# Attention and quantised feed-forward block on one core: another order of the shared work, and another split of the PSUM banks

## What is computed

```python
xn = layernorm(x)
Q, K, V = xn @ W_q.T, xn @ W_k.T, xn @ W_v.T      # 16 heads of 16
scores = rope(Q) @ rope(K).T * DH ** -0.5          # causal
heads = softmax(scores) @ V
attn = heads @ W_o.T
xq, wq = fake_quant_fp8(xn), fake_quant_fp8(weight)   # one scale per tensor
out = x + attn + (xq @ wq.T + bias)
```

## The kernel before

| slot | items | slot | items |
|---|---|---|---|
| 0, 2 | v0; v1 | 11 | fin0 |
| 1, 7 | mt1; mt2 | 12 | at2, mt3 |
| 3 to 6 | o0; o1; o2; o3 | 13 | qk2 |
| 8 | at0, qk0 | 14 | fin1, at3 |
| 9 | at1 | 15, 16 | qk3; fin2, mt0 |
| 10 | qk1 | 17, 18, 19 | none; fin3; none |

## Time and profile before

### The profile page before, as it was taken

The page is one execution under the profiler, slowest core; times in us unless marked ns, Lnnn a source line. Parts: engine busy times, 40 slices in busy tenths (PEclk is TensorE's granted clock), DMA queues, the critical chain, the costliest instruction groups (busy, mean ns, idle before and its releaser), DMA issues.

```text
span 438.0 us, 9484 instructions
## 1 busy us (share of the span) xinstructions
PE 384.9 (88%) x2990; PEld 205.9 (47%) x2990; DVE 355.3 (81%) x1380; ACT 290.6 (66%) x487; POOL 245.4 (56%) x266
## 2 busy tenths in 40 slices
PE   7998987878879988998899898989899998898886
PEld 7685543333434544454445444545445433353335
DVE  3899679999888988898888979887989797879104
ACT  3529538567765777587866776676677677669751
POOL 5444263365559548556666666676666565245750
PEclk9996979999989999999999999999999999999999
DMA  8944032302503143302630262018031613020111
GB/s 280 307 146 71 1 94 79 73 2 97 123 0 75 52 157 62 75 27 94 148 75 1 98 171 61 15 52 216 15 62 49 183 38 74 2 99 4 49 49 49
DMA packets 27810, 36.40 MB, mean 83 GB/s; under 512 B 3984, under 2 KB 25872, under 8 KB 26320
## 3 DMA queue, kind: packets, MB, share of 16 engines
q1 hardware_dynamic: 27760, 35.79, 30.2%
HBM read 22.94 MB, written 12.58 MB: 81 GB/s over the span
## 4 chain that ended last, share of the span: by engine, by line
PE 63%; ACT 16%; DVE 10%; issue 7%; POOL 2%; DMA 1%; ACTq 0%; POOLq 0%; SPq 0%; DVEq 0%
PE o_ps L1047 15%; ACT prob L803 12%; PE st_ps L943 9%; PE m_ps L927 9%; PE m_ps L1005 7%; PE m_ps L982 7%; PE s_ps L962 5%; DVE scratch L657 4%; PE m_ps L989 2%; PE s_ps L899 2%; DVE prod L605 2%; DMA q_st<-shift 1%; PE m_ps L1013 1%; DVE prod L604 1%; DVE amax L593 1%
## 5 line engine op out<-in xcount | busy, mean ns | idle before, releaser
L803 ACT ACTIVATE prob<-st_ps,exp_scale 128x512 f32<-128x512 f32 x320 | 202.9, 689 | 98.9 <-PE st_ps L943 98.2
L657 DVE CUSTOM_DVE_ANT_0 scratch<-s_ps,causal 128x512 bf16<-128x512 f32 (+3 forms) x512 | 221.3, 484 | 35.8 <-PE s_ps L962 33.8
L510 POOL TENSOR_SCALAR_AFFINE_SELECT prob<-prob 128x512 f32<-128x512 f32 (+1 forms) x160 | 90.1, 565 | 147.4 <-ACT prob L803 147.3
L943 PE MATMUL st_ps<-q_st,k_st 50*128 50x128 f16 (+3 forms) x512 | 108.9, 303 | 35.4 <-ACT prob L803 26.9
L962 PE MATMUL s_ps<-k_st,q_st 48*128 48x512 f16 (+3 forms) x512 | 109.7, 306 | 4.7 <-DVE rowmax L657 4.4
L943 PEld LDWEIGHTS st_ps<-q_st,k_st 50*128 50x128 f16 x512 | 35.2, 94 | 121.1 <-ACT prob L803 74.6
L1047 PE MATMUL o_ps<-prob,v_sb 128*17 128x512 f32 (+3 forms) x1024 | 82.8, 441 | 1.7 <-POOL prob L510 0.9
L962 PEld LDWEIGHTS s_ps<-k_st,q_st 48*128 48x128 f16 x512 | 34.5, 95 | 15.9 <-DVE rowmax L657 9.0
L657 DVE DVE_READ_ACCUMULATOR2_ANT rowmax<- 128x1 f32 x512 | 41.1, 80 | 0.0
L1047 PEld LDWEIGHTS o_ps<-prob,v_sb 128*17 128x17 f32 x1024 | 23.2, 97 | 30.0 <-issue 23.0
L982 PE MATMUL m_ps<-wv_sb,xnT 128*128 128x256 f32 x128 | 33.7, 408 | 1.5 <-ACT v_sb L810 1.3
(11 more groups left out here) (130 smaller groups left out, 493.5 us busy)
## 6 DMA issues: line engine op xcount, KB each, us to landing
qk_parts<-parts SPq DMA_DIRECT2D x14, 512.0 KB, 3.6
xnT<-x_dram SPq DMA_DIRECT2D x8, 512.0 KB, 8.5
q_st<-qk_parts SPq DMA_DIRECT2D x15, 256.0 KB, 4.2
k_st<-qk_parts SPq DMA_DIRECT2D x15, 256.0 KB, 4.6
x_res<-x_dram SPq DMA_DIRECT2D x7, 512.0 KB, 3.4
out_dram<-x_res SPq DMA_DIRECT2D x7, 512.0 KB, 3.0
q_st<-qk_parts SPq DMA_DIRECT2D x17, 128.0 KB, 3.2
k_st<-qk_parts SPq DMA_DIRECT2D x17, 128.0 KB, 4.9
```

The costliest lines, as they stand in the source:

```text
L510: eng.affine_select(out=ap, in_=ap, compare_op=ALU.is_ge, fill=0.0, base=0, pattern=pat, channel_multiplier=-1).then_inc(masked, 1)
L657: eng.tensor_tensor_reduce(scratch[:, at % 3, col:col + w], s_ps[at % 3][:, col:col + w], causal[:, T - w:T], 1.0, NEG, ALU.add, ALU.max, ...
L803: eng.activation(prob[u][:, half * T:(half + 1) * T], st_ps[ST_BANK[2 * s + half]][:, :], ACT.Exp, scale=exp_scale[:, 0:1]).then_inc(exp_d ...
L943: mm = eng.matmul(st_ps[ST_BANK[i]][:, col:col + T - kb * P], k_rows(n, h, ROWS + SHIFT, slice(kb * P, (kb + 1) * P)), q_rows(n, h, ROWS + ...
```

## The change

Shared items get new slots, the attention transposes go two to a bank (`at` 0 and 1), `fin` 2 and 3 of a batch move to slots 2 and 5 of the batch after next (for batch 6, LAST_FINS keeps all four in batch 7), and v 0 of a batch moves into the last slot of the batch before. In slots 0 to 19 taken modulo 20 the items now stand like this:

| slot | items | slot | items |
|---|---|---|---|
| 0 | v1 | 10 | qk0 |
| 1 | mt1 | 11 | mt3 |
| 2 | fin2 | 12 | qk1 |
| 3 | o0 | 13 | at1 (row blocks 2, 3) |
| 4 | o1 | 14 | fin1 |
| 5 | fin3 | 15 | qk2 |
| 6 | mt2 | 16 | mt0 |
| 7 | o2, at0 (row blocks 0, 1) | 17 | qk3 |
| 8 | o3 | 18 | none |
| 9 | fin0 | 19 | v0 |

st_ps gets 3 banks and s_ps 2, so an attend waits for the exponential three banks back and a compare for the maxima two banks back. v_sb, x_res and xq are doubled and attnT holds all four row blocks. The steps of CHAIN, of the quantisation, of the residual and of SyncE's stores move with the items.

```diff
-OFFSETS = {("v", 0): 0, ("mt", 1): 1, ("v", 1): 2, ("o", 0): 23, ("o", 1): 24, ("o", 2): 25, ("o", 3): 26, ("mt", 2): 7,
-           ("at", 0): 28, ("qk", 0): -32, ("at", 1): 29, ("qk", 1): -30, ("fin", 0): 31, ("at", 2): 32, ("mt", 3): 12,
-           ("qk", 2): -27, ("fin", 1): 34, ("at", 3): 34, ("qk", 3): -25, ("fin", 2): 36, ("mt", 0): -4, ("fin", 3): 38}
+OFFSETS = {("v", 0): -1, ("v", 1): 0, ("mt", 0): -4, ("mt", 1): 1, ("mt", 2): 6, ("mt", 3): 11,
+           ("o", 0): 23, ("o", 1): 24, ("o", 2): 27, ("at", 0): 27, ("o", 3): 28, ("at", 1): 33,
+           ("fin", 0): 29, ("fin", 1): 34, ("fin", 2): 42, ("fin", 3): 45,
+           ("qk", 0): -30, ("qk", 1): -28, ("qk", 2): -25, ("qk", 3): -23}
+LAST_FINS = {("fin", 0): 29, ("fin", 1): 30, ("fin", 2): 34, ("fin", 3): 35}
-CHAIN = {("rotate", 0): -29, ("high", 0): -28, ("low", 0): -26, ("write", 0): -25, ("rotate", 1): -24, ("high", 1): -23,
-         ("low", 1): -21, ("write", 1): -20, ("read", 0, 0): -19, ("read", 0, 1): -16, ("read", 1, 0): -12,
-         ("read", 1, 1): -11}
+CHAIN = {("rotate", 0): -27, ("high", 0): -26, ("low", 0): -24, ("write", 0): -22, ("rotate", 1): -22, ("high", 1): -21,
+         ("low", 1): -19, ("write", 1): -17, ("read", 0, 0): -16, ("read", 0, 1): -14, ("read", 1, 0): -8,
+         ("read", 1, 1): -6}
...
-ST_BANK = [i % 2 for i in range(HALVES)]
-ST_BEFORE = [i - 2 for i in range(HALVES)]
+ST_BANKS, S_BANKS = 3, 2
...
-    first, last, loop = (24, 25, 26, 27, 28), (6, 7, 11, 12, 14), (16, 17, 21, 22, 24)
+    first, last, loop = (24, 25, 26, 27, 28), (6, 7, 11, 12, 14), (16, 18, 20, 23, 25)
...
-        v_sb = sb("v_sb", [P, NQ, H, VW])
+        v_sb = sb("v_sb", [P, 2, NQ, H, VW])
-        scratch = sb("scratch", [P, 3, T], BF16)
+        scratch = sb("scratch", [P, S_BANKS, T], BF16)
-        attnT = sb("attnT", [P, 2, NC, P])
-        x_res = sb("x_res", [P, NQ, D])
-        xq = sb("xq", [P, NC, T], BF16)
+        attnT = sb("attnT", [P, NQ, NC, P])
+        x_res = sb("x_res", [P, 2, NQ, D])
+        xq = sb("xq", [P, 2, NC, T], BF16)
...
-                for g, off in enumerate((-3, 2, 8, 13)):
+                for g, off in enumerate((-3, 2, 7, 12)):
...
-                n = batch_at(slot, 39)
-                if n is not None and n < NB - 1:
-                    store(n)
+                for n in range(NB - 1):
+                    if slot == SLOTS * n + (47 if n < NB - 2 else 37):
+                        store(n)
...
-                n = batch_at(slot, -34, 2)
+                n = batch_at(slot, -32, 2)
                 if n is not None:
                     split_x(n)
...
-                n = residual_at(slot, 29, 17)
+                n = residual_at(slot, 27, 17)
...
-                    wait_past(eng, exp_done, HALVES * n + ST_BEFORE[i] + 1)
+                    wait_past(eng, exp_done, HALVES * n + i - ST_BANKS + 1)
...
-                    wait_past(eng, max_done, ITEMS * n + (ITEMS_UP_TO[f - 3] if f >= 3 else ITEMS_UP_TO[f - 3] - ITEMS))
+                    wait_past(eng, max_done, ITEMS * n + (ITEMS_UP_TO[f - S_BANKS] if f >= S_BANKS else ITEMS_UP_TO[f - S_BANKS] - ITEMS))
...
+            def turn_two(n, i, bank):
+                turn_attn(n, 2 * i, bank, 0)
+                return turn_attn(n, 2 * i + 1, bank, D)
```

More of the change, by code:

```diff
@@ L68, in schedule @@
     order = {key: i for i, key in enumerate(OFFSETS)}
-    items = [(EARLY[kind, k] if (kind, n) == ("qk", 1) else SLOTS * n + off, order[kind, k], kind, n, k)
+    items = [(EARLY[kind, k] if (kind, n) == ("qk", 1) else
+              SLOTS * n + (LAST_FINS[kind, k] if (kind, n) == ("fin", NB - 2) else off), order[kind, k], kind, n, k)
              for (kind, k), off in OFFSETS.items() for n in range(NB) if (kind, n) != ("qk", 0)]
@@ L218, in xq_of, with residual_of @@
         def xq_of(n):
-            return xq if n < NB - 1 else parts[:, 0, 0].bitcast(BF16)
+            return xq[:, n % 2]
+        def residual_of(n):
+            return x_res[:, n % 2]
         def q_rows(n, h, rows, cols):
@@ L244, in attention_ffn_block @@
                         for i in range(2)]
-        wf_sb = xq[:, :, :].rearrange("p c t -> p (c t)").bitcast(F32).rearrange("p (c n) -> p c n", c=NC)
-        st_ps = [pb(f"st_ps{i}", [P, T]) for i in range(2)]
-        s_ps = [pb(f"s_ps{i}", [P, T]) for i in range(3)]
+        wf_sb = xq[:, 0].rearrange("p c t -> p (c t)").bitcast(F32).rearrange("p (c n) -> p c n", c=NC)
+        st_ps = [pb(f"st_ps{i}", [P, T]) for i in range(ST_BANKS)]
+        s_ps = [pb(f"s_ps{i}", [P, T]) for i in range(S_BANKS)]
         o_ps = pb("o_ps", [P, T])
@@ L253, in attention_ffn_block @@
         first_ps = m_ps + s_ps[0:2]
-        tail_o, tail_at = s_ps + m_ps[0:1], m_ps[1:2] + st_ps + [o_ps]
+        tail_o, tail_at = s_ps + m_ps, st_ps + [o_ps]
         turn_ps = (st_ps[0], o_ps)
@@ L808, in copy_v @@
                 if i == 0:
-                    wait_past(eng, pv_done, 8 * n)
-                eng.copy(v_sb[:, 2 * i:2 * i + 2, :, 0:DH],
+                    wait_past(eng, pv_done, 8 * (n - 1))
+                eng.copy(v_sb[:, n % 2, 2 * i:2 * i + 2, :, 0:DH],
                          bank[:, :].rearrange("p (k h w) -> p k h w", k=2, h=H)).then_inc(v_copied, 1)
@@ L817, in copy_heads, with copy_at, copy_last_at @@
                 eng.copy(heads[:, g, :], o_ps[:, :]).then_inc(heads_copied, 1)
[L819 to L828 removed]
+            def copy_at(n, i, bank):
+                eng.wait_ge(full["at"], 2 * n + i + 1)
+                wait_past(eng, full["fin"], 4 * (n - 1) + 2 * i + 2)
+                eng.copy(attnT[:, 2 * i:2 * i + 2], bank[:, :].rearrange("p (q c n) -> p q c n", q=2, c=NC))\
+                   .then_inc(at_copied, 1)
+            def copy_last_at(qb, bank):
+                n = NB - 1
+                eng.wait_ge(full["at"], 2 * n + qb + 1)
+                eng.wait_ge(full["fin"], 4 * n)
+                eng.copy(attnT[:, qb], bank[:, 0:D].rearrange("p (c n) -> p c n", c=NC)).then_inc(at_copied, 1)
             nw = NC * D
@@ L848, in _ @@
                     eng.wait_ge(w_max_done, 8)
-                n = batch_at(slot, -35, 2)
+                n = batch_at(slot, -34, 2)
                 if n is not None:
@@ L877, in _ @@
                     copy_v(n, i, shared["v", n, i])
-                for n, qb in [(n, qb) for _, n, qb in shared_at(slot, "at")]:
-                    copy_at(n, qb, shared["at", n, qb])
+                for n, i in [(n, i) for _, n, i in shared_at(slot, "at")]:
+                    copy_at(n, i, shared["at", n, i])
                 for g in range(NG - 1):
@@ L898, in keep_busy @@
                 for _ in range(count):
-                    eng.matmul(s_ps[2][:, 0:P], ident[:, :], ident[:, :], start=True, stop=True)
+                    eng.matmul(st_ps[2][:, 0:P], ident[:, :], ident[:, :], start=True, stop=True)
             def turn_rows(n):
@@ L1004, in output_of_attn @@
                 for c in range(NC):
-                    mm = eng.matmul(bank[:, 0:D], attnT_of(n, qb)[:, c, :], wo_sb[:, c, :],
+                    mm = eng.matmul(bank[:, 0:D], attnT[:, qb, c, :], wo_sb[:, c, :],
                                     start=(first and c == 0), stop=(not first and c == NC - 1))
```

64 lines of the change are left out of this document (22 added, 42 removed).

## The result

The change makes the kernel **slower**: 455.58 us median of four runs (453.69 to 457.13) against 440.38 for the kernel before, run beside it on the same chip (439.63 to 443.50). The ratio is 1.033, with a 95% interval of 1.026 to 1.040. The forecast was 424, its range 412 to 437; the time lies on the other side of no change, next to the 454 of the fourth rival, but mostly not by that rival's mechanism.

A forecast was written before the change was run, and what follows sets the result against it. TensorE was taken to bound the kernel, standing still 5.75 us of each 46.15 us batch. Start +2.5, batch 1 -3.0, batches 2 to 5 -8.8, batch 6 -2.9, batch 7 -3.4 sum to -15.6 from 439.77: 424 us, range 412 to 437.

The forecast's parts named there:

- fourth rival: Every slot: two s_ps banks couple VectorE and TensorE, a batch takes 48.6 us, in all 454 us; chance 0.12.
- I take +2.5, bounds +1 and +5: Start and batch 0: back-to-back v items and two s_ps banks leave VectorE idle, slot 19 ends 2.4 us later.
- It gains 2.2 too: Batch 1: the steady batch's 2.2 us gain plus 0.8 for fin 2 and 3 leaving it, 3.0 in all.
- only remove waits: Whole kernel: doubling xq, x_res and v_sb was costed at nothing, as it could only take waits away.
- 43.95 us a batch: Batches 2 to 5: 40.4 us of TensorE work plus 3.55 of new stops; 2.2 less each, 8.8 for four.
- so ScalarE's hold on TensorE goes: Steady batches: a third st_ps bank and even items remove all of the 5.75 us standstill except the listed new stops.
- Together 2.55: Steady batch: compares wait for VectorE's maxima, 1.1 us after slots 10, 12, 15, 1.0 in slot 19, 0.45 after slot 4.
- The wait in slot 8: Slot 8: first_block waits for o_ps behind ScalarE's heads copy, itself held until o 3; 0.7 us of standstill.
- The collision: Slot 18: VectorE's exponent step qe meets GpSimd's rotation; 0.3 us a batch, bounds 0 and 1.
- second rival: Slot 18 of six batches: the port lock decides, 1.2 us in place of 0.3, in all 429 us; chance 0.10.
- -2.9 and -3.4: Batch 6 forecast at 38.7 us, 2.9 less; batch 7 at 37.1, 3.4 less, with the tail from 424.4 us unchanged.
- The marks I had set: Confirming: st_ps hold under 2 us, slot 20 2 to 3 later. Refuting: batches above 45.5, s_ps waits above 5, qk0 waiting.

The follow-up runs named there:

- e3: Changed kernel with ScalarE's copy of v in slot 20 moved ahead of its four weight scalings: 451.48 us, 1.020 of the kernel before.
- e7: Changed kernel on the old banks (two st_ps, three s_ps), with slot 20's v copy first and batch 0's quantisation early: 435.85 us, 0.988 of the kernel before.
- e9: e7 with batch 0's residual loaded in slot 4 and biased in slot 13, before the exponents: 435.25 us, 0.987 of the kernel before.
- e11: e7 with the attends from slot 150 on cycling over all five score banks: median 439.24 us over ten runs, 0.983 of the kernel before.
- e12: e7 with the edits of e9, e10 and e11 together: 432.79 us, 0.985 of the kernel before.
- e10: e7 with o 2 and o 3 one slot earlier and at 0 one later: 438.24 us, 0.994 of the kernel before.
- e13: e7 with the edits of e9 and e11, without that of e10: 432.02 us, 0.977 of the kernel before.
- e6: e5 on the old banks, two st_ps and three s_ps: 437.09 us, 0.990 of the kernel before.
- e2: Changed kernel on the old banks (two st_ps, three s_ps), so the new order alone: 445.54 us, 1.009 of the kernel before.
- e8: Changed kernel with the first matmul of each attend of batch 0 issued twice: 454.69 us, 1.031 of the kernel before.
- e4: Changed kernel with batch 0's last two quantisation steps moved to slot 26, ahead of the residual's addition and split_x: 449.73 us, 1.017 of the kernel before.
- e5: Changed kernel with the edits of e3 and e4 and batch 0's v items in slots 0 and 2: 447.16 us, 1.015 of the kernel before.
- two-by-two: Old and new order, each on old and new banks; steady batch 46.2 (both old), 47.5 (e1), 44.2 (e2), 45.4 us (both new).
- e14: Changed kernel with VectorE's exponent step qe moved from slot 18 back to slot 17: 460.71 us, 1.044 of the kernel before.
- e1: Kernel before with only the banks moved (three st_ps, two s_ps), old order kept: 453.69 us, 1.026 of the kernel before.

## Why the prediction was wrong, point by point

1. **The start and batch 0: the step that failed most by size.** I wrote "I take +2.5, bounds +1 and +5". Slot 20 is reached at 122.26 in place of 108.36, 13.9 later. Three things are in it. ScalarE's copy behind the scalings is 3.7 (e3 reaches slot 20 at 118.56). The banks are 2.9 to 3.9 (e3 against the 114.7 to 115.7 of e7, e9, e11 and e12, which also have the copy first and a slow first v). The other 6.3 to 7.3 is the new order in an execution with a slow first v; in e10 and e13, where that product was fast, slot 20 is reached at 111.3, only 3.0 later than before. So 3.3 to 4.4 of it can come and go with the execution, which I had not priced. The kernel before had a slow first v (3.78), and I counted with that figure, so like against like the order costs 6.3 to 7.3; that my +2.5 is near the 3.0 of the fast kind is luck. Which waits make up the 6.3 to 7.3 no run splits. Of the cause I looked at the wrong half: the v items back to back, which e6 against e7 shows to be worth nothing on the old banks. I had two s_ps banks leave VectorE dry twice (0.35 and 1.25) and put no stop of TensorE behind VectorE in batch 0, where VectorE is the fuller engine: matmuls for s_ps wait 9.3 us there, in 20 places, weight loads 15.0, against 1.7 and 2.8 before, and the run of value products at 80.73 takes 2.76 us where the four steady ones take 1.49. My roll by slots priced every later item at the higher level. The grant of 0.83 isn't the banks' alone: on the old banks batch 0 had 0.86 in e2 and e7 and 0.82 in e9, with 49.4 us. How much of the loss is waiting and how much is clock stays open (e8).

2. **Batch 1: "It gains 2.2 too", 3.0 in all, was +6.4, and the stop of 3.64 in front of it +3.6.** I moved `fin` 0 of batch 0 five slots forward, as the list has it, and didn't follow xq back through GpSimd's queue; nor did I look at what stands ahead of copy_v in slot 20 on ScalarE. Both stops were readable from the diff: double buffers "only remove waits", I wrote, but a product moved forward waits for whoever makes its operand. e3 (-4.1) and e4 (-5.9) measured them. Without these two stops the changed kernel's bank split would still lose (e5, 1.015), and with them mended the other split wins (e7, 0.988): both misses were needed for the 3.3%. For the sign either was enough: with the stops and the old banks (e2) the kernel is slower too, 1.009.

3. **Steady batches: right in direction, short in size.** "43.95 us a batch" was 45.4; the gain of 8.8 was 3.1. The step that failed is "so ScalarE's hold on TensorE goes": I priced that hold at nearly all of 5.75, and the two-by-two shows that the third st_ps bank gave less than the loss of the third s_ps bank took (a net loss of 1.2 to 1.3), while the order, which I had only as a condition, gave 2.0. With two st_ps banks and the new order the batch takes 44.2, close to my number, by the other part of the change.

4. **The compares with two s_ps banks.** "Together 2.55" was about right in kind: by slot starts the stops are 0.79 behind slot 4, 0.46, 0.53 and 0.47 behind the projections and 1.1 in slot 19, 3.35 in all. But TensorE is also late by 0.64 in slot 8 beyond the heads' 0.73, and by 0.28 in slots 0 and 6: 5.0 us against 3.55.

5. **The wait in slot 8: exact.** 0.7 predicted, 0.73 measured, each batch. That removing it pays would have been wrong: in e10 the next wait is longer (1.18). `split_x`, costed at nothing with a thin cover, made qk0 wait nowhere in the changed kernel's steady batches; in e4 and e7 (batch 1) and in e10 (every batch) it did.

6. **The collision: right in size.** "I take 0.3 a batch, bounds 0 and 1": VectorE pays 0.92 in a batch (the median of eight is 1609 ns; before, one case stood out), and by e14's distance between the two v items 0.43 of it is on TensorE's path. At 311.34 GpSimd began a rotation of 1.27 us, at 311.55 the step began and took 1.61: the rest of the rotation, 1.06, and 0.69 of its own make 1.75, a little more than was measured. GpSimd's next rotation, begun at 312.56, took 1.71 in place of 1.27. The Trainium skill, "SBUF — State Buffer", the section on its two physically separate sides, has this as an exclusive lock of a port pair, between VectorE in a two-port mode and GpSimd; this trace agrees. The second rival, which made it decide, fell.

7. **Batches 6 and 7.** -2.9 and -3.4 were -0.4 and, with the tail, -0.3. In e2 they are -1.4 and +2.2. Batch 6's count failed as the steady one did, since its stops are the same. Batch 7 up to the last slot is shorter (39.07 against 40.50), and the tail, which I called unchanged, is 0.9 longer (14.5 against 13.6) at a clock of 0.87. No run tested these two by themselves.

8. **The marks I had set.** Batches above 45.5 would have refuted me: they are 45.4. The s_ps waits above 5: 4.8 for weight loads and 1.7 for matmuls, each under the mark and together over it. The hold under 2: it is 5.2, a plain miss, and the sign that the third bank would not give what I had it give. "Slot 20 reached 2 to 3 us later": 13.9, the mark that showed most of the loss. qk0 does not wait for `split_x`.

9. **The fourth rival** gave 454 by 48.6 us in every batch. Its mechanism, two s_ps banks tying VectorE to TensorE, is real: e1 shows it at 47.5 a batch, and it is 2.4 to 4.8 of the 8.4 of batch 0 (51.9 in e3 against 49.1 to 49.5 in e7, e9, e11 and e12; 55.0 against e2's 50.2). In the changed kernel it costs 1.2 a steady batch, where the rival had 2.4 above the kernel before. The time fits the rival, the places don't.
